# Evictions ahead of clamps, maxima and scales in a linear-attention and ternary FFN layer

## The reference

```python
def act_quant(x):     # per token: scale = 127 / max|x|, round, back
def weight_quant(w):  # one scale per matrix: s = mean|w|; clip(round(w/s), -1, 1) * s
def h_bitlinear(x, w):
    xq = act_quant(fwht(x))          # Walsh-Hadamard along the row
    wq = weight_quant(w)
    return jnp.einsum('bsh,oh->bso', xq, wq)
gate = h_bitlinear(hidden_states, w_gate)     # (8192, 2048)
up = h_bitlinear(hidden_states, w_up)
return h_bitlinear(jax.nn.silu(gate) * up, w_down)
```

## Time and profile before

| what | value |
|---|---|
| median of 3 runs | 2512.76 us |
| lowest and highest run | 2364.22, 2557.56 us |
| the profiled execution | 2365.61 us |
| its span on the slowest core (core 3) | 2364.1 us |
| spans of the 8 cores | 2348.9 to 2364.1 us |
| granted TensorE clock, mean of a core | 0.976 to 0.981 |
| TensorE busy | 2181.8 us (92%) |
| ScalarE busy | 1271.1 us (54%) |
| VectorE busy | 1202.1 us (51%) |

### The profile page before, as it was taken

The page is one execution under the profiler, slowest core; times in us unless marked ns, Lnnn a source line. Parts: engine busy times, 40 slices in busy tenths (PEclk is TensorE's granted clock), DMA queues, the critical chain, the costliest instruction groups (busy, mean ns, idle before and its releaser), DMA issues.

```text
span 2364.1 us, 30891 instructions; the slowest of 8 cores (2348.9 to 2364.1 us)
## 1 busy us (share of the span) xinstructions
PE 2181.8 (92%) x10648; PEld 1013.8 (43%) x10648; DVE 1202.1 (51%) x1677; ACT 1271.1 (54%) x1340; POOL 78.3 (3%) x140
## 2 busy tenths in 40 slices
PE   4899989999798787999999999999997899999998
PEld 2444435554343333444444444444443344444443
DVE  4664143545555656444444444425686868660125
ACT  4634664434355656877776555536556854750241
POOL 1000000000000000000000000000000000100000
PEclk9999999999999899999999999999999999999999
DMA  8778798878792566999889989875566546822346
GB/s 282 219 233 248 199 235 240 234 175 226 164 231 90 162 242 217 315 337 336 310 285 331 314 306 314 299 254 185 181 222 228 173 147 204 282 84 76 107 160 214
DMA packets 92342, 535.59 MB, mean 227 GB/s; under 512 B 10845, under 2 KB 11101, under 8 KB 37918
## 3 DMA queue, kind: packets, MB, share of 16 engines
q1 hardware_dynamic: 62574, 441.23, 55.2%
q0 software_dynamic: 13488, 63.02, 12.0%
q10 hardware_dynamic: 16128, 29.37, 4.0%
HBM read 529.48 MB, written 37.75 MB: 240 GB/s over the span
## 4 chain that ended last, share of the span: by engine, by line
PE 68%; DVE 11%; issue 7%; ACT 7%; DMA 6%; ACTq 0%; DVEq 0%; SPq 0%; POOLq 0%
PE ps L1016 29%; PE ps L1024 15%; PE ps L965 5%; PE ps L797 4%; PE ps L818 4%; PE ps L902 2%; ACT wfb L1800 2%; DVE P L1473 2%; PE ps L763 2%; DMA wfb<-wut 2%; PE ps L688 2%; DMA wfb<-wgt 2%; PE ps L738 1%; ACT P L1847 1%; DVE P L1553 1%
## 5 line engine op out<-in xcount | busy, mean ns | idle before, releaser
L1016 PE MATMUL ps<-xq,tq 128*128 128x512 bf16 x4096 | 902.8, 382 | 27.8 <-DVE tq L1364 8.2
L1016 PEld LDWEIGHTS ps<-xq,tq 128*128 128x128 fp8e4 x4096 | 402.1, 99 | 522.5 <-issue 52.1
L1800 ACT ACTIVATE wfb<-wfb,is_col 128x2048 int8<-128x2048 f32 x192 | 381.7, 1994 | 178.9 <-DMA wfb<-wut 83.1
L1601 ACT ACTIVATE wfb<-wfb 128x2048 f32<-128x2048 f32 x173 | 329.2, 1903 | 132.6 <-DMA wfb<-wdt 52.2
L1024 PE MATMUL ps<-tq,P 128*128 128x512 fp8e4 x1664 | 369.6, 383 | 7.1 <-ACT P L1811 4.1
L1364 DVE TENSOR_SCALAR tq<-wfb 128x2048 fp8e4<-128x2048 int8 x176 | 215.1, 1223 | 267.2 <-ACT wfb L1800 169.2
L1024 PEld LDWEIGHTS ps<-tq,P 128*128 128x128 bf16 x1664 | 164.0, 99 | 208.7 <-issue 16.8
L1560 DVE SCALAR_TENSOR_TENSOR P<-ps,s,P 128x512 f16<-128x512 f32 x128 | 96.0, 750 | 250.5 <-PE ps L1016 250.3
L1898 ACT ACTIVATE sig_scr<-P 128x512 f16<-128x512 f16 x128 | 79.6, 627 | 184.3 <-DVE P L1553 183.5
L965 PE MATMUL ps<-P,hi_t 128*128 128x512 f16 x640 | 148.3, 381 | 21.1 <-ACT P L1840 14.3
L1553 DVE TENSOR_TENSOR P<-ps,bc_g 128x512 f16<-128x512 f32 x128 | 87.9, 687 | 70.8 <-PE ps L1016 70.8
(11 more groups left out here) (200 smaller groups left out, 1926.3 us busy)
## 6 DMA issues: line engine op xcount, KB each, us to landing
wfb<-wgt SPq DMA_DIRECT2D x128, 1024.0 KB, 8.2
wfb<-wut SPq DMA_DIRECT2D x128, 1024.0 KB, 9.4
wfb<-wdt SPq DMA_DIRECT2D x128, 1024.0 KB, 7.0
tq<-tern_d ACTq DMA_DIRECT2D x64, 256.0 KB, 2.7
tern_gu<-tq POOLq DMA_DIRECT2D x48, 256.0 KB, 7.2
tq<-tern_gu ACTq DMA_DIRECT2D x48, 256.0 KB, 4.3
xin<-x_pre SPq DMA_DIRECT2D x8, 1024.0 KB, 8.7
wk_f<-wk SPq DMA_DIRECT2D x8, 1024.0 KB, 16.1
```

The costliest lines, as they stand in the source:

```text
L1016: mm = t.matmul(out=ps[k % 4][:, 0:512], lhsT=tq[e.slot][:, j, :], rhs=xq[g][:, j, :], start=(j == 0), stop=(j == 15))
L1601: s.activation(out=w, in_=w, func=AF.Abs, accum_out=scol[:, j.col:j.col + 1]).then_inc(s_wab, 1)
L1800: s.activation(out=w.bitcast(I8T)[:, 0:D], in_=w, func=AF.Copy, scale=is_col[:, m:m + 1]).then_inc(s_wsc, 1)
```

## The change

On VectorE the maxima leave `beside` for a function of their own. In steps 0 to 287 the order becomes: `beside` without maxima, weight sums, `gate_up`, maxima, clamps. On ScalarE, scales of tiles for the `tq` buffers come after `beside_first`, and scales of tiles made ahead come last in their step, after the loads of copies. No instruction is added or removed, and none changes its shape.

```diff
--- before.py
+++ after.py
@@ -1512,9 +1512,6 @@
                 for p in range(len(x.pairs)):
                     if x.t_pair[p] == step:
                         butterfly(x, p)
-                for j in range(1, x.nq):
-                    if x.t_max[j] == step:
-                        max_take(x, j)
                 if step == x.t_fold:
                     fold(x)
                 if step == x.t_col:
@@ -1526,6 +1523,12 @@
                 for i in range(x.nq):
                     if x.t_q[i] == step:
                         quantise(x, i)
+
+        def maxima(step):
+            for x in XF:
+                for j in range(1, x.nq):
+                    if x.t_max[j] == step:
+                        max_take(x, j)
 
         pending = []
 
@@ -1562,6 +1565,7 @@
 
         for step in range(WO0, 0):
             beside(step)
+            maxima(step)
             if step == WO0 + 4:
                 weight_scales(0)
             if step == -7:
@@ -1575,13 +1579,15 @@
                     weight_sums(n)
                 if step == STEP_SUM[n] + 1:
                     weight_scales(n)
+            if step < NGU:
+                gate_up(step)
+            maxima(step)
             for j in jobs_of_step(step):
                 if j.entry:
                     clamp(j.entry)
                 elif j.early:
                     clamp_early(j.early)
             if step < NGU:
-                gate_up(step)
                 continue
             d = step - NGU - 17
             if d >= 0 and d % 16 == 0:
@@ -1882,12 +1888,11 @@
             beside_last(step)
         n_gate = 0
         for step in range(NSTEP):
-            for j in jobs_of_step(step):
-                if j.eng == "t":
-                    scale(j)
             beside_first(step)
             for j in jobs_of_step(step):
-                if j.eng == "a":
+                if j.entry:
+                    scale(j)
+                elif j.eng == "a":
                     weight_abs(j)
             if step < NGU:
                 if STEPS_GU[step][0] == "g":
@@ -1906,6 +1911,9 @@
             beside_last(step)
             for e in copies_after(step):
                 load_copy(e)
+            for j in jobs_of_step(step):
+                if j.early:
+                    scale(j)
         for g in range(NG):
             for tok in range(CPG):
                 s.wait_ge(s_dnb, 24 + 4 * g + tok + 1)
```

## The result

The changed kernel took 2346.38 us, the median of 6 runs (2344.26 to 2612.59), beside 2440.19 us for the kernel before (6 runs, 2363.62 to 2574.9). The ratio is 0.9913, with a 95% interval of 0.9898 to 0.9928: the kernel became faster, by 20 us. The forecast was 0.990.

What follows compares the result with a forecast made beforehand. TensorE, busy 92% of the span, was taken as the bound, so only its idle time pays. Terms -6.9 - 20.6 + 0 + 5 - 1.9 = -24.4 us from 2365.61 gave 2341.2 us, ratio 0.990, range 2325 to 2358.

Steps and rivals of the forecast that it cites:

- rival 3: Steps 5 to 26 and 150 to 177: both loops open fully, -74 us, kernel 2292; chance 0.08.
- rival 2: Steps 9 to 22: lockstep of VectorE and ScalarE returns, -6 in place of -20.6 us, kernel 2356; chance 0.18.
- Part 1: Steps 5 to 8: Hadamard evictions ahead of scales end TensorE's wait for the fourth bank, -6.9 us.
- part 5: Steps 178 to 223: Hadamard evictions ahead of scales shorten waits, a later scale takes some back, -1.9 us.
- the first gain: Steps 5 to 8: 1.9 us gained besides the three shortened periods.
- Part 2: Steps 9 to 28: evictions ahead of clamps open the loop, each engine goes at its own load, -20.6 us.
- the walk: Both engines' queues followed through steps 9 to 22: evictions 62.5 us apart in place of 82.06, -19.6 us.
- Part 3: Steps 24 to 127: clamps and loads come later but TensorE has no idle time, 0 us.
- Rival 1: Steps 24 to 127: the weight stream runs dry and TensorE waits, +51 to +84 us; chance 0.12.
- Part 4: Steps 150 to 172: scales of tiles made ahead move behind the sigmoid, gate steps stay a closed loop, +5 us.
- the bound of +3: Steps 178 to 223: the upper end given for the forecast of -1.9 us.

Runs made afterwards that it cites:

- the first four experiments: VectorE's order alone, 0.9866; ScalarE's Hadamard evictions ahead of scales alone, 1.0024; changed kernel with scales of tiles made ahead in front, 0.9841; change in steps 0 to 127 only, 0.9884.
- the third experiment: The changed kernel with scales of tiles made ahead back at the start of ScalarE's step: 2328.46 us, ratio 0.9841 to the kernel before.
- the fifth experiment: The changed kernel with ScalarE's old order from step 128 on and scales of tiles made ahead first everywhere: 2328.35 us, ratio 0.985 to the kernel before.

## Why the prediction was right and where it was wrong

**The time was right, and the bound of the chances was wrong.** 2341.2 us were forecast beside 2346.38, a ratio of 0.990 beside 0.9913. The step that failed is the last one of the text on chances: "Within 2% is about what a measurement of this kernel can't tell from no change: 47 us". The spread of 193 us between the three runs shown, and a round 2%, were taken for the resolution. But fourteen of the sixteen runs of the kernel before that stood beside the first four experiments lie between 2362.42 and 2366.77, the interval of the result is 3.5 us to either side, and the prediction's own range of 2325 to 2358 lay wholly below the 2365.61 it was made against. By its own terms "faster, and told apart" had a chance of 0.8 or more: the forecast (0.62), rival 3 (0.08) and most of rival 2, whose -10 us would also have been told apart. It put 0.86 on no change that can be told. The measured change, 0.87% of the time, is six times the half-width of its interval (0.15%).

**The sum was close in part by luck.** -24.4 us were forecast for the span and -21.8 came. Part 1 gave 1.1 more than forecast, by a term that was not costed, and part 5 lost 3.1 against its forecast, by a term that was wrong; parts 2 to 4 were off by 0.2 to 0.4 each.

**Part 1, near in sum only (-6.9; -8.0 measured).** The period fell to 6.9 us, and the three periods gave 5.0 as forecast; the first gain was 0.2 and not 1.9. The other 2.8 lie in steps 0 to 4, which the prediction did not cost: there `beside_first` moves copies of the transposed input ahead of the scale as well, which alone costs 7.5 us, and gains only together with VectorE's half.

**Part 2, right (-20.6; -20.2 from step 8 to 30).** The predicted distances 4.7, 4.7, 5.9, 2.1, 4.3, 4.2, 4.2, 5.7, 2.1, 6.1, 5.0, 4.9, 4.3, 4.3 became 4.5, 4.5, 5.7, 2.1, 4.5, 4.2, 4.2, 5.3, 2.1, 6.2, 5.1, 4.9, 4.3, 4.5. (The second list is that of seven of the eight cores.) The lengthened clamps and the shortened absolute values show why the walk worked in the steps that they touch: before, what was added on VectorE and what was taken from ScalarE both moved the evictions in full; after, an operation did so only on the more loaded engine. One sign was missed: ScalarE's wait for evictions was to fall below 10 us and fell from 33.7 to 16.0. None of it lies in steps 12 to 15, where ScalarE sets the pace; that the rest costs nothing was not tested.

**Part 3, right (0; -0.2).** No wait of TensorE for a tile after step 19, and a buffer less costs 1 us over steps 24 to 148. Rival 1, at 0.12, was further away than it looked: even the experiment made to bring it about did not.

**Part 4, right (+5; +5.3), with errors that cancel.** The eviction of step 158 is 2.8 us later (2.2 predicted) and the fold 4.4 later after it (4.0). The clamp of step 172 gives 2.4 back: its wait of 1.21, which was counted, and its own 1.14, which was not, as the eviction is now ahead of all of it. Steps 172 to 175 add 0.5 that was not costed. The closed loop through the scale behind the sigmoid is shown by the third experiment: with that scale in front, the stage is 18 us shorter. The prediction saw the loss but not that the rest of the change could have won 13 us there.

**Part 5, wrong in sign (-1.9; +1.2, and +2.3 up to step 208).** From step 175 to the end the cores take 527.1 to 528.7 us before and 527.6 to 530.9 after; the kernels that have the order of before there take 527.0 and 527.3 in the mean (the change up to step 127, the kernel before with five buffers), those with the whole change 529.0 and 530.0, so the sign holds. The waits of the earlier trace rows were taken to be worth their length. They are not (and the first of them, which was to lose 1.9, lost 0.2): TensorE resumes in step 208 when ScalarE evicts, ScalarE stands behind absolute values, and these behind VectorE's chain of butterflies, whose first maximum comes 174.0 us after the eviction of step 175 before, and 176.2 after. What TensorE wins in the Hadamard steps it waits off there. The later scale delays that chain, the bound of +3 that the prediction kept.

**Rival 2** is excluded by the 62.2 us. **Rival 3** did not come, but part of it can be had: in the experiment with VectorE's half, 50.2 us from step 158 to 172 beside the 48.3 of fourteen units.

What stays open: why the gain of 1.2 us that the third and the fifth experiment should differ by doesn't appear in their times. It is below what the runs resolve.

## What to carry to other kernels

When two engines wait for each other once a step, write down the loop with its durations and ask of each moved instruction whether it is in it; then let each engine's own load give the new pace, stage by stage, as the bound can change engine within ten steps. Moving work on one engine only can lengthen the loop that the same move opens when both engines are changed, so a change of order is tried half by half. And the size that can be told apart comes from how closely most runs agree, not from the distance to the few that stand apart.
